# The 5x5 taps of keys and values, moved from TensorE to GpSimd

## What is computed

```python
def _L0_conv_ref(x, w_qkv, w_dw, w_pw, w_proj, ...):
    qkv = conv2d(x, w_qkv)                                        # 1x1, 64 -> 192
    agg = conv2d(qkv, w_dw, padding=SCALE // 2, groups=3 * TOTAL) # 5x5, each channel alone
    agg = conv2d(agg, w_pw, groups=3 * HEADS)                     # 1x1 in groups of 8
    qkv_ms = jnp.concatenate([qkv, agg], axis=1)
    out = relu_linear_att(qkv_ms)
    out = conv2d(out, w_proj)
    inv = bn_gamma / jnp.sqrt(bn_var + BN_EPS)
    return out * inv[...] + (bn_beta - bn_mean * inv)[...]
...
x = x + _L0_conv_ref(_gn(x), ...)    # _gn: normalised over pairs of channels
```

## Time and profile before

| what | us |
| --- | --- |
| three runs of the kernel | 948.5, 948.72, 945.65 (median 948.5) |
| the profiled execution, its own time | 947.5 |
| its span in the trace | 945.6 |
| PE busy | 843.2 (89%) |
| DVE busy | 574.3 (61%) |
| ACT busy | 456.3 (48%) |
| POOL busy | 205.0 (22%) |
| mean granted TensorE clock, 1.00 is full speed | 0.962 |

### The profile page before, as it was taken

One profiled execution on the slowest core, in us unless ns is written; L12 is line 12 of the kernel. 1 busy time (PEld: TensorE's weight loads), 2 busy tenths in 40 slices (PEclk: granted clock), 3 DMA queues, 4 the chain that ended last, 5 costly groups with the idle time before them and its releaser, 6 DMA issues.

```text
span 945.6 us, 24504 instructions
## 1 busy us (share of the span) xinstructions
PE 843.2 (89%) x10312; PEld 591.4 (63%) x10312; DVE 574.3 (61%) x1678; ACT 456.3 (48%) x764; POOL 205.0 (22%) x274
## 2 busy tenths in 40 slices
PE   9887898999999999999999999999888889879776
PEld 8775565567666766676667666766555556546553
DVE  5545534674588458845885588548864763642546
ACT  1002326463556256536553665356555655525754
POOL 1002100220124013411241124112411241131122
PEclk9999669999999999999999999999999999988988
DMA  8200000100000100000011001000010000030000
GB/s 216 38 7 1 1 7 4 38 21 26 21 21 22 26 21 22 21 27 5 24 34 27 3 22 38 21 1 21 24 37 21 21 21 21 25 76 21 1 1 24
DMA packets 25901, 24.41 MB, mean 26 GB/s; under 512 B 14752, under 2 KB 20768, under 8 KB 25664
## 3 DMA queue, kind: packets, MB, share of 16 engines
q1 hardware_dynamic: 25792, 22.85, 9.1%
HBM read 20.21 MB, written 2.62 MB: 24 GB/s over the span
## 4 chain that ended last, share of the span: by engine, by line
PE 54%; DVE 21%; ACT 13%; issue 5%; DMA 3%; POOL 2%; SPq 1%; DVEq 0%; POOLq 0%; ACTq 0%
PE ring L957 6%; PE side_a L649 5%; PE pv L977 5%; PE ring L906 5%; PE pv L995 4%; ACT pr L1212 4%; PE heads L896 3%; PE side_a L658 2%; DVE img L1418 2%; PE heads L939 2%; PE heads L878 2%; PE side_c L754 2%; PE ring L924 2%; DVE toks L1690 1%; PE ring L914 1%
## 5 line engine op out<-in xcount | busy, mean ns | idle before, releaser
L1212 ACT ACTIVATE pr<-ring 128x1024 f32<-128x1024 f32 (+1 forms) x128 | 120.9, 944 | 100.0 <-PE ring L924 61.0
L957 PE MATMUL ring<-kq 64*128 64x256 f32 (+2 forms) x1280 | 136.4, 341 | 4.1 <-ACT kq L1264 4.0
L957 PEld LDWEIGHTS ring<-kq 64*128 64x128 f32 x1280 | 95.4, 190 | 37.3 <-issue 20.1
L1256 ACT ACTIVATE kq<-ring 128x896 f32<-128x896 f32 x64 | 58.8, 919 | 76.0 <-PE ring L906 76.0
L1690 DVE TENSOR_REDUCE toks<-heads 128x2 f32<-128x512 f32 x64 | 44.2, 691 | 79.8 <-PE heads L924 79.4
L1715 DVE SCALAR_TENSOR_TENSOR ob<-pv,all_gates,scale 128x256 f32<-128x256 f32 x96 | 46.3, 482 | 63.3 <-PE pv L995 29.2
L582 POOL TENSOR_TENSOR toks<-ta,tb 128x128 f32<-128x128 f32 (+1 forms) x96 | 40.0, 437 | 166.1 <-DVE tb L1681 166.1
L1264 ACT ACTIVATE kq<-ring 128x256 f32<-128x256 f32 x64 | 24.6, 384 | 99.4 <-PE ring L914 98.8
L906 PE MATMUL ring<-early,toks 128*128 128x128 f32 x448 | 63.8, 284 | 8.2 <-ACT pr L1212 8.0
L545 POOL TENSOR_TENSOR oT<-ob 128x256 f32<-128x256 f32 x32 | 23.3, 728 | 212.1 <-DVE ob L1715 212.1
L1695 DVE TENSOR_REDUCE toks<-heads 128x4 f32<-128x512 f32 x64 | 44.1, 689 | 37.0 <-PE heads L939 36.6
(11 more groups left out here) (378 smaller groups left out, 1777.9 us busy)
## 6 DMA issues: line engine op xcount, KB each, us to landing
scale<-branch_scale SPq DMA_DIRECT2D x128, 96.0 KB, 2.2
late<-in_late SPq DMA_DIRECT2D x1, 2158.5 KB, 8.5
branch_scale<-rden SPq DMA_DIRECT2D x32, 64.0 KB, 1.5
xin<-in_x SPq DMA_DIRECT2D x16, 64.0 KB, 2.2
pr<-in_prep SPq DMA_DIRECT2D x1, 602.0 KB, 3.9
y<-ob SPq DMA_DIRECT2D x8, 64.0 KB, 1.9
kq<-in_masks SPq DMA_DIRECT2D x1, 480.0 KB, 9.1
toks<-in_final SPq DMA_DIRECT2D x1, 434.0 KB, 4.4
```

The costliest lines, as they stand in the source:

```text
L957: m = pe.matmul(ring[:, j, at:at + nq], kq[rows, k, key0:key0 + P], kq[rows, k, Q + q_:Q + q_ + nq], start=r % 2 == 0, stop=at > P)
L1212: act.activation(out, in_, ACT.Exp, scale=SCALE).then_inc(S("exp_done"), 1)
L1256: act.activation(kq[:, k, :], flat[:, 0:WIDE], ACT.Copy).then_inc(S("turned"), 1)
```

## The change

For every image but the first, keys and values no longer take their 5x5 from composed weights on PE. In the period before the image's own front a third generator, `before(n, image)`, runs on four engines in slots of its own, counted in quarter rounds (`FIRST_BEFORE_AT` for image 1, `BEFORE_AT` for the others):

- DVE computes the group statistics of the next image into buffers of their own, normalises into `xg` and forms the residual, in one of two buffers by turns (`xs_of`).
- PE projects `xg` to 128 keys and values with one matmul of 256 columns into bank `SB_`.
- ACT copies the result into a bordered plane `kvpad`, which lies in the place of `wc_kv`.
- POOL takes the square root of the norm and then does 25 taps of 256 columns: each multiplies a window of `kvpad` by a weight per partition (`tensor_scalar`) and adds it to `kvsum` (`tensor_tensor`). One tap is multiplied ahead of the addition of the one before. The 25 taps are spread over slots; in `BEFORE_AT` 15 of them stand in quarter rounds 41 to 70, the rest before.

In the image's own front (`tapped`) PE waits for all taps, does the queries' 5x5 as before, and mixes keys and values with two matmuls of `kvsum` tokens with `pw_kv`, in the place of the two transposes. DVE copies the four windows from `xg`. The copy to `kv1` goes for these images. The fillers ahead of the convolution and ahead of the turn of `xn2` go too; before that turn PE now waits for the next plane's `padded`. SP loads the pixels of image 1 and the tap weights `pw_kv` and `dwk` ahead of the rounds, and those of image n + 2 in round 4 of front n. Some semaphores are merged (`late`, and the three of the last routing into `route_out` and `route_ready`), and three buffers share places with others (`den0` and `rec0` with `x1`, `cmp_` and `cmq_` with `hm`). The first image goes the old way (`composed`).

```diff
-        den0, rec0 = xg, kv1
         x1 = sb("x1", [P, T])
+        den0 = rec0 = x1
+        pst = sb("pst", [P, 2, 6])
+        pmv = sb("pmv", [P, 2, 2])
+        pgm = sb("pgm", [P, 2])
+        pgt = sb("pgt", [P, 2])
+        wcf = wc_kv[:, :, :].rearrange("p n m -> p (n m)")
+        kvpad = wcf[:, 0:PITCH * PITCH].rearrange("p (h w) -> p h w", h=PITCH)
+        at = PITCH * PITCH
+        kvsum = wcf[:, at:at + T]
+        tap_kv = [wcf[:, at + (1 + i) * T:at + (2 + i) * T] for i in range(2)]
+        at += 3 * T
+        pw_kv = wcf[:, at:at + P]
+        dwk = wcf[:, at + P:at + P + 26]
...
-        cmp_, cmq_ = keep5[:, 0:NT, :], keep5[:, NT:2 * NT, :]
+        cmp_, cmq_ = hm[:, 0:NT, :], hm[:, NT:2 * NT, :]
...
+        def xs_of(image):
+            return (xs, kv1)[image % 2]
+
+        TAPS = [(4 * dy + dx if dx < 4 else 20 + dy, dy, dx) for dy in range(5) for dx in range(5)]
...
+        FIRST_BEFORE_AT = dict(
+            PE=(15, 16),
+            DVE=(5, 6, 18),
+            ACT=(24,),
+            POOL=(14, 34, 35, 35, 37, 38, 38, 41, 42, 42, 42, 43, 44, 45, 45, 45, 46, 48, 49, 50, 52, 53, 54, 62, 67, 70),
+        )
+        BEFORE_AT = dict(
+            PE=(6, 13),
+            DVE=(3, 9, 10),
+            ACT=(13,),
+            POOL=(9, 11, 15, 17, 19, 20, 37, 39, 39, 40, 41, 47, 50, 50, 51, 51, 53, 58, 62, 62, 62, 62, 65, 68, 70, 70),
+        )
+
         ORDER = ('filled', 'scored', 'early', 'maxed', 'late', 'turned', 'weighed')
+
+        QUARTER = dict(filled=0, early=1, late=2, weighed=3)
...
-        def run(name, fronts, backs, restart=None, ahead=None, **hooks):
+        def run(name, fronts, backs, pres, restart=None, ahead=None, **hooks):
 
             for t in TIMES:
                 if restart is not None and t % ROUNDS == 0:
                     restart()
                 for part in ORDER:
+                    for n in range(B - 1):
+                        at = 4 * (t - FRONT_AT[n]) + QUARTER.get(part, -1000)
+                        for _ in range((BEFORE_AT if n else FIRST_BEFORE_AT)[name].count(at)):
+                            next(pres[n], None)
...
+            sp.wait_ge(S("x_free"), 1)
+            for half_ in range(2):
+                sp.dma_start(xin[half_ * C:(half_ + 1) * C, :], x_in[1]).then_inc(S("x_loaded"), 16)
+            sp.wait_ge(S("conv5"), 1)
+            a = po["pw_kv"][0]
+            sp.dma_start(pw_kv, prep_in[:, a:a + P]).then_inc(S("tap_weights"), 16)
+            sp.dma_start(dwk, prep_in[:, 0:26]).then_inc(S("tap_weights"), 16)
...
-                for n in range(B - 1):
-                    if t == FRONT_AT[n] + 3:
-                        sp.wait_ge(S("x_free"), n + 1)
+                for n in range(B - 2):
+                    if t == FRONT_AT[n] + 4:
+                        sp.wait_ge(S("x_free"), n + 2)
                         for half_ in range(2):
-                            sp.dma_start(xin[half_ * C:(half_ + 1) * C, :], x_in[n + 1])\
+                            sp.dma_start(xin[half_ * C:(half_ + 1) * C, :], x_in[n + 2])\
                                 .then_inc(S("x_loaded"), 16)
...
+            def before(n, image):
+                rsqrt(n, pgt[:, 1:2], pgt[:, 0:1], "gn1_var", "gn1_rstd")
+                yield
+                pool.wait_ge(S("tap_weights"), 16 * 2)
+                pool.wait_ge(S("padded"), image)
+                pool.wait_ge(S("conv5"), image)
+                kinds = ((kvpad, H, tap_kv, kvsum, dwk),)
+                taps_before = (image - 1) * len(TAPS) * len(kinds)
...
+                def scaled(i, x):
+                    at, dy, dx = TAPS[i]
+                    pad, rows, taps, sums, weights = kinds[x]
+                    out = sums if i == 0 else taps[i % 2]
+                    if i > 2:
+                        pool.wait_ge(S("tap_summed"), sums_before + (i - 2) * len(kinds) + x + 1 - len(kinds))
+                    nc.gpsimd.tensor_scalar(out.rearrange("p (h w) -> p h w", h=rows), pad[:, dy:dy + rows, dx:dx + W],
+                                            weights[:, at:at + 1], None, ALU.mult).then_inc(S("tapped"), 1)
+
+                def summed(i, x):
+                    _, _, taps, sums, _ = kinds[x]
+                    pool.wait_ge(S("tapped"), taps_before + i * len(kinds) + x + 1)
+                    if i > 1:
+                        pool.wait_ge(S("tap_summed"), sums_before + (i - 1) * len(kinds) + x + 1 - len(kinds))
+                    if i:
+                        nc.gpsimd.tensor_tensor(sums, sums, taps[i % 2], ALU.add).then_inc(S("tap_summed"), 1)
...
+                if len(kinds) == 1:
+                    scaled(0, 0)
+                for i in range(len(TAPS)):
+                    if len(kinds) == 1:
+                        if i + 1 < len(TAPS):
+                            scaled(i + 1, 0)
+                    else:
+                        scaled(i, 0)
+                        scaled(i, 1)
+                    for x in range(len(kinds)):
+                        summed(i, x)
+                    yield
+
             def front(n):
-                rsqrt(n, gt[:, 1:2], gt[:, 0:1], "gn1_var", "gn1_rstd")
+                if n == 1:
+                    rsqrt(n, gt[:, 1:2], gt[:, 0:1], "gn1_var", "gn1_rstd")
                 yield
...
-            def front(n, mean_bank=SA):
+            def before(n, image):
+
                 after(n, "gn1_stats")
-                if n > 1:
-                    after(n - 1, "selT")
+                if image > 1:
+                    pe.wait_ge(S("padded"), image - 1)
+                pe.matmul(SB_[:, 2 * T - 2:2 * T], cst("pairmean"), pmv[:, 0, :], start=True, stop=True)\
+                    .then_inc(S("gn1_mean"), 1)
+                yield
+                after(n, "gn1_done")
+                m = pe.matmul(SB_[:, 0:T], cst("w_kv0"), xg[:, :], start=True, stop=True)
+                m.then_inc(S("unpadded"), 1)
+                yield
+
+            def tapped(n, image):
+
+                yield
+                busy_until(n, "gn1_done")
+                yield
+                after(image, "selT")
+                pe.wait_ge(S("tap_summed"), 24 * image)
+                after(n, "windows")
+                for up in range(2):
+                    pe.matmul(SA[C * up:C * up + C, T + P:2 * T], cst("w_q0"), half_window(up, 0, 2, 2), start=True,
+                              stop=True)
+                for i, (copy, dy, dx) in enumerate(PAIRS5):
+                    for up in range(2):
+                        m = pe.matmul(SA[C * up:C * up + C, T:T + P], wc_q[:, i, :], half_window(up, copy, dy, dx),
+                                      start=(i == 0), stop=(i == 12))
+                for t in range(NT):
+                    m = pe.matmul(SA[:, t * P:(t + 1) * P], kvsum[:, t * P:(t + 1) * P], pw_kv, start=True, stop=True)
+                m.then_inc(S("conv5"), 1)
+                yield
+                busy_until(n, "kv1_copied")
+                after(n, "kv1_copied")
+                for t in range(NT):
+                    m = pe.matmul(SA[:, T + t * P:T + (t + 1) * P], xg[:, t * P:(t + 1) * P], cst("w_kv0"),
+                                  start=True, stop=True)
+                m.then_inc(S("kv1_turned"), 1)
+                yield
+
+            def composed(n, mean_bank):
+
+                after(n, "gn1_stats")
                 pe.matmul(mean_bank[:, 0:2], cst("pairmean"), mv[:, 0, :], start=True, stop=True)\
                     .then_inc(S("gn1_mean"), 1)
                 yield
                 busy_until(n, "gn1_done")
-                if n > 2:
-                    after(n, "gn1_var")
...
                 for i, (copy, dy, dx) in enumerate(PAIRS5):
                     pe.matmul(SA[:, 0:T], wc_kv[:, i, :], window(copy, dy, dx), start=(i == 0), stop=(i == 12))
                 yield
-                if n == 1:
-                    pe.wait_ge(S("conv_weights"), 6)
+                pe.wait_ge(S("conv_weights"), 6)
...
+            def front(n, mean_bank=SA):
+                yield from composed(n, mean_bank) if n == 1 else tapped(n, n - 1)
...
-                busy(4, SB_)
+                pe.wait_ge(S("padded"), min(image + 4, B - 1))
                 after(n, "xn2")
                 turn_twice("xn2_turned")
...
+            def before(n, image):
+                act.wait_ge(S("unpadded"), image)
+                if image > 1:
+                    act.wait_ge(S("tap_summed"), 24 * (image - 1))
+                act.activation(kvpad[:, 2:2 + H, 2:2 + W], SB_[:, 0:T].rearrange("p (h w) -> p h w", h=H), ACT.Copy)\
+                    .then_inc(S("padded"), 1)
+                yield
...
+            def before(n, image):
+                dve.wait_ge(S("x_loaded"), image * 32 + 32)
+                group_stats(xin, 1, pst, pmv)
+                yield
+                group_var(n, SB_[:, 2 * T - 2:2 * T], 1, pgm, pgt)
+                yield
+                after(image, "kv1_turned")
+                if image == 1:
```

(49 more changed lines are left out.)

35 lines of the change are left out of this document (16 added, 19 removed).

## The result

The changed kernel took 1005.5 us, median of four runs (1001.21 to 1006.86), against 948.57 for the kernel before. The ratio is 1.0608, 95% interval 1.057 to 1.0646: 6% slower. The forecast was 935.5, with 918 to 961 as its range, so it was wrong in sign.

The account below looks back on a forecast made before the run. PE's order was taken to bound steady periods; 5.5 us saved per image, less POOL's lateness and the first period's loss, gave a 12 us gain, 947.5 - 12 = 935.5 us, range 918 to 961.

Parts of the forecast that it names:

- 132 - 100p: Total gain in us over images 1 to 7, p being one POOL tap pair; 12 us at p = 1.20.
- Above stands the two-input addition: POOL's multiplication by a scalar taken as 0.40 us, between the memset's 0.34 and the addition's 0.73.
- Rival C: POOL's multiplication as dear as an addition, felt in 15 taps behind n3; deciding from 0.52 us, 968 at 0.73; chance 0.19.
- All three signs: Forecast wrong if multiplication exceeds 0.5 us, clock is 0.5 after the new waits, or DVE releases PE before the queries.
- A term put at nothing: POOL taken as free for n3 at 480.74 us, as in the old profile; no later start was charged.
- DVE's hold-ups: POOL and DVE blocking each other behind n3: 1.2 us, between 0 and 4.5; plus 0.45 for DVE instructions held up.
- Rival E: Held-up DVE instructions delay the maxima PE's banks wait for; at 2 us more per image, 947 us; chance 0.09.
- Image 2: Its taps fall into the sparse second period and fit on POOL, so it gains the full 5.5 us.
- the base gain: Gain per image before POOL's lateness, from PE's 13 pairs, filler and wait leaving: 5.5 us.
- the first period's loss: Image 1's steps and 25 taps run serially beside image 0's front: 25p - 20.2, or 9.8 us lost.
- the place behind n3: 15 taps behind POOL's n3 step make it late for PE's queries: 15p - 15.7, 2.3 us at p = 1.20.
- Rival D: Granted clock falls in PE's new waits, so the queries' 3.03 us take twice that; 953 us; chance 0.12.

Follow-up runs that it names:

- two_taps: Changed kernel with only two of the 25 taps done, every other step kept; 916.6 us.
- first_ten: Changed kernel with only the first ten taps done, all in slots ahead of n3; 934.6 us.
- last_fifteen: Changed kernel with only the last 15 taps done, all in slots behind n3; 993.2 us.
- placed: Changed kernel with POOL's slots for images 2 to 7 moved: 17 taps into gaps ahead of n3, 8 behind it; 982.2 us.
- tensor_mult: Changed kernel with each tap's multiplication a two-input tensor_tensor with broadcast weight instead of tensor_scalar; 974.5 us.
- placed_tensor_mult: Changed kernel with both the moved slots (17 taps ahead of n3, 8 behind) and the two-input multiplication with broadcast weight; 981.0 us.
- split_dve15: Changed kernel with ten taps on POOL ahead of n3 (two-input multiplication) and 15 on DVE, PE mixing two sums; 957.0 us.

## Why the prediction was wrong

The sum was 132 - 100p. With the measured pair, p = 1.72, it gives -40 us, 987.5. Part by part, from the starts of the queries in the two timelines:

| part | before | after | by the sum at p = 1.72 | measured |
| --- | --- | --- | --- | --- |
| start to image 1's queries | 68.18 | 91.54 | 25p - 20.2 = +22.8 | +23.4 |
| to image 2's | 73.06 | 72.91 | -5.5 | -0.2 |
| to image 3's | 85.85 | 92.62 | 15p - 21.5 = +4.3 | +6.8 |
| images 4 to 7, sum of four | 386.35 | 410.01 | 4 x (15p - 21.2) = +18.4 | +23.7 |
| behind image 7's queries | 332.2 | 332.2 | 0 | 0 |
| sum | 945.6 | 999.3 | +40.0 | +53.7 |

**The step that failed** is "Above stands the two-input addition" in the part on POOL. Nothing in the trace made an addition an upper bound for a multiplication of one tensor: the two are different instructions, and tensor_scalar takes 0.934 us where the range ended at 0.73. It is the term of the sum that was mis-sized, 1.20 taken and 1.72 measured, and it accounts for 52 of the 65.7 us by which the sum was off. Rival C named the mechanism and its place, and its break-even at 0.52; it was given 0.19, at a price still too low. The GPSIMD Engine Reference of the Trainium skill (section 3.1), by the 1.03 cycles an element that the prediction cites, spoke for the low price; no row of tensor_scalar here agrees with it. All three signs that the prediction named for being wrong came: the multiplication is over 0.5 us, the clock is at 0.5 behind a new wait (the token mean's), and DVE releases PE at the queries in the period shown.

**A term put at nothing** is the start of n3. The sum left it where it was and counted what stands behind it: 12.5 + 15 x 1.72 + 1.2 = 39.5 us, and 38.7 were measured. But n3 itself starts 63.3 to 64.2 us behind the queries, against 59.7 to 60.7 before (61.0 to 62.2 in two_taps). What makes it late is not settled: first_ten, with the same ten taps ahead of n3, has it at 61.9 to 62.7.

**DVE's hold-ups** were mis-sized too: 1.2 us plus 0.45 taken, 3.4 to 6.9 us of DVE's busy time a period measured in last_fifteen, placed and tensor_mult (69.0 to 72.6 against 65.65). The slots matter: the ten taps of first_ten, ahead of n3, add only about 1 us (66.74). By SBUF — State Buffer of the Trainium skill (Who interferes with whom) the prediction had reckoned 4.5, for the two-input instructions behind n3 alone. The measured sizes lie near it, but they hold one-input instructions as well, so they do not confirm that count. Rival E had them delaying the maxima, with its gain gone at 2 us more a period. How much of the 7.8 us by which the five later periods are above the sum is theirs is not shown. In placed_tensor_mult, at full clock and with POOL waiting for DVE at n3 and ln4's root, they are the likeliest cause of what is left. In split_dve15 what is left stands beside DVE's own taps, which make up most of the 8 to 9 us in its column.

**Image 2** was said to fit. It lost the 5.5 us of its gain: its taps stand ahead of image 1's second group norm in POOL's queue, 4.7 us late there by the rows above. With 12.3 us of lateness, in placed, its period grows by 9.1 us more. The prediction looked at what waits for the taps, and not at what is queued behind them.

**Right** were the base gain (5.0 against 5.5), the first period's loss with all 25 taps (+23.4 us by 22.8, and +14.1 by 15 at tensor_mult's pair of 1.41), the place behind n3, the token mean as a spot where part of the lateness shows early, and the old fillers. With ten taps the formula fails: first_ten loses 6.1 us where it gives a gain of 3.0, because POOL's roots for the running image wait behind the taps.

**Rival D** came in part: the clock falls, at the token mean and not at the queries. In the changed kernel the chain that it lengthens ends together with POOL's taps, and holding the clock up alone gives 1.7 us a period. Where POOL is earlier the clock shows beside the hold-ups: 95.3 us at full clock in placed_tensor_mult, 99.2 to 100.9 at 0.92 to 0.95. The cheaper tap in better slots did not bring a period below 95.

## What to carry to other kernels

Before work is moved to an engine that has never run its instruction in this kernel, the price has to be taken as open on the upper side as well: the nearest other instruction bounds nothing. An idle engine's time is not free where its instructions hold up a busy one's: look at the busy engine's column with the work in and out. Where two things end together, taking one away shows little of either: compare single periods with and without each, and not totals alone. And where one queue serves several images, ask which short step of the running image will stand behind the long row of the next.

## What the runs showed that was not expected

- On POOL a multiplication by a scalar per partition took 0.934 us for 128x256, with a constant 0.856, and as a two-input multiplication with a broadcast weight 0.627.
- A memset on POOL holds up one-input instructions of DVE: 1.69 us became 3.27.
- At 440 to 444 us of the changed kernel the granted clock fell from 1.00 to 0.5 although PE was busy there, behind a stretch with waits of 1.07 us for the third attention's norm and 0.7 for the selection.
- In two_taps, where POOL is not late, a steady period with the granted clock at 0.50 for 10 us took 95.6 us instead of 90.6 to 91.5.
